# Whole and half tiles in two expert layers, early mixture tiles beside the row scatters, and a transposing load of the mixture's rows

## What is computed

```python
gate = sigmoid(h @ Wh.T + z_t @ Wz.T + b)                 # recurrence over 256 steps
h = tanh(h * leak + gate * z_t)
mask = one_hot(top_k(softmax(xt @ gate_w + gate_b), 2)).sum(1)      # first expert layer, E = 8, F = 1024
x = x + einsum('eth,te->th', relu(xt @ w1[e] + b1) @ w2[e] + b2, mask)
shared = (silu(x @ sw1.T) * (x @ sw3.T)) @ sw2.T          # mixture: shared layer of 512
routed = sum over the top 2 of gate_e * gelu(x @ rw1[e].T) @ rw2[e].T     # 8 experts of 128
y = (shared + routed) / 3
x = x + quantised_ffn(y)                                  # scales from maxima over all tokens
```

## Time and profile before

| | |
|---|---|
| median of the runs | 1201.23 us |
| profiled execution | 1204.75 us, span 1202.9 us |
| TensorE | 1023.2 us busy (85%), weight loads 805.0 us |
| VectorE, ScalarE, GpSimd | 823.5, 548.2, 389.3 us busy |
| first expert layer | 377.6 to 790.3 us |
| router, shared units, row scatters | 790.3 to 912.6 us |
| mixture tiles | 912.6 to 1036.4 us |
| sum of results | 1036.4 to 1087.5 us |

### The profile page before, as it was taken

How to read it: one execution, slowest core, us unless ns; L and a number is a source line. 1 busy time by engine, 2 the same in 40 slices (tenths; PEclk the granted TensorE clock), 3 DMA queues, 4 the chain that set the end, 5 groups by cost and what they waited for, 6 DMA issues and landing times.

```text
span 1202.9 us, 30907 instructions
## 1 busy us (share of the span) xinstructions
PE 1023.2 (85%) x10073; PEld 805.0 (67%) x10085; DVE 823.5 (68%) x2840; ACT 548.2 (46%) x1736; POOL 389.3 (32%) x428
## 2 busy tenths in 40 slices
PE   6777777777777999999999999967678999667898
PEld 5656656566565888888888888854355787433355
DVE  5676777776776778985555555528664777777887
ACT  4555555555554333333333333343425767114376
POOL 1002112111123666243333333315773667202000
PEclk9999999999999999999999999979898999978999
DMA  8313323233233578555444443374246998530024
GB/s 231 102 58 103 90 89 103 83 99 102 76 107 107 88 140 165 101 84 67 66 66 57 62 64 60 59 200 161 89 140 207 281 291 280 198 121 0 1 36 105
DMA packets 127354, 136.49 MB, mean 113 GB/s; under 512 B 62337, under 2 KB 102146, under 8 KB 127042
## 3 DMA queue, kind: packets, MB, share of 16 engines
q1 hardware_dynamic: 104770, 93.34, 29.4%
q0 software_dynamic: 22464, 41.61, 15.3%
HBM read 74.43 MB, written 58.70 MB: 111 GB/s over the span
## 4 chain that ended last, share of the span: by engine, by line
PE 66%; DVE 14%; ACT 9%; issue 5%; POOL 3%; DMA 3%; SPq 0%; DVEq 0%; POOLq 0%; ACTq 0%
PE ps L1395 17%; PE ps L1405 17%; PE ps L646 10%; PE ps L2011 8%; DVE ps L1940 6%; PE ps L2016 5%; ACT work L1864 4%; ACT ps L1859 4%; POOL mrows L1331 2%; DVE imax L1253 2%; PE ps L1981 2%; PE ps L731 2%; PE ps L1162 1%; PE ps L1167 1%; PE ps L1133 1%
## 5 line engine op out<-in xcount | busy, mean ns | idle before, releaser
L1423 ACT ACTIVATE lane<-ps,b_now 128x256 f32<-128x256 f32 x312 | 147.6, 473 | 260.3 <-PE ps L1395 248.4
L1395 PE MATMUL ps<-lane,W 128*128 128x256 f16 x1872 | 213.1, 274 | 0.9 <-issue 0.9
L1405 PE MATMUL ps<-W,lane 128*128 x1872 | 210.7, 273 | 0.2 <-DVE lane L1498 0.2
L1395 PEld LDWEIGHTS ps<-lane,W 128*128 x1872 | 183.9, 98 | 24.0 <-issue 1.7
L1405 PEld LDWEIGHTS ps<-W,lane 128*128 128x128 f16 x1872 | 182.8, 98 | 22.1 <-issue 0.8
L1572 POOL DMA_INDIRECT results<-lane,dest x78 | 125.2, 1605 | 216.7 <-DVE lane L1486 180.5
L2011 PE MATMUL ps<-work 128*128 128x16 f16 x2048 | 98.8, 177 | 86.1 <-ACT work L1864 85.4
L2011 PEld LDWEIGHTS ps<-work 128*128 128x128 f16 x2048 | 76.1, 106 | 137.8 <-ACT work L1864 136.3
L1498 DVE TENSOR_TENSOR lane<-lane 128x256 f16<-128x256 f32 x312 | 133.1, 427 | 10.8
L1542 POOL DMA_INDIRECT rows<-work,slot_of x64 | 63.1, 987 | 156.4 <-DVE ps L1940 152.4
L1496 DVE CAST lane<-lane 128x256 f16<-128x256 f32 x312 | 93.5, 300 | 20.5 <-ACT lane L1423 20.5
(11 more groups left out here) (260 smaller groups left out, 1660.2 us busy)
## 6 DMA issues: line engine op xcount, KB each, us to landing
W<-mrows SPq DMA_DIRECT2D x39, 260.0 KB, 3.9
stage<-rweights SPq DMA_DIRECT2D x39, 256.0 KB, 3.7
stage<-in_w1T SPq DMA_DIRECT2D x16, 512.0 KB, 3.8
stage<-in_w2T SPq DMA_DIRECT2D x16, 512.0 KB, 4.1
b_now<-in_b SPq DMA_DIRECT2D x39, 128.0 KB, 2.9
work<-in_zT SPq DMA_DIRECT2D x32, 128.0 KB, 2.3
results<-in_xn SPq DMA_DIRECT2D x32, 128.0 KB
W<-results SPq DMA_DIRECT2D x8, 512.0 KB, 4.5
```

The source lines that it names most:

```text
L1395: last = pe.matmul(ps[:, f % 4, 0:ST], of_e(W1[:, bass.ds(e, 1), a, k, f * P:(f + 1) * P]), xT[:, p, b, k], start=(i == 0 and k == 0), sto ...
L1405: last = pe.matmul(ps[:, 4 + q, 0:D], hid[:, a, f, q * P:(q + 1) * P], of_e(W2[:, bass.ds(e, 1), b, f]), start=(i == 0 and f == 0), stop=( ...
L1423: act.activation(v4[:, f % 4], ps[:, f % 4, 0:ST], ACT.Relu, bias=b1_now[:, p, f:f + 1], scale=A_SCALE / W_SCALE).then_inc(l1_v, 1)
```

## The change

Both expert layers take 32 tiles of 256 rows and then 7 of 128 (`UNITS_MAX` = 71 half tiles of work, at most), the half ones written out after the loop; the table operations give each tile its room in units of 128 rows, 28 operations for the late part instead of 17, and the mixture uses the same two tables: the first 16 tiles after step 2, the rest three operations at a time among the tiles. Each group has its own row buffer. `mixT` is filled by a transposing DMA and `mtail` by a load of its own; the transposes on TensorE and their copy on ScalarE are gone. The pad writes stand in SP's tile loop behind tile 2. The steps hold 6, 9, 12 and 14 units, the tiles 45 (two per tile for the first seven, then one), 10 are behind. `x1` comes in 16 pieces, four in flight. The sum comes after all units, with two loads per group; the last group's shared outputs are read by ScalarE.

```diff
 PAIRS = 2 * N
-SLOT_TILES = (PAIRS + E * (ST - 1)) // ST
+HT = ST // 2
+UNITS_MAX = (PAIRS + E * (HT - 1)) // HT
+WHOLE_TILES = PAIRS // ST
+HALF_TILES = UNITS_MAX - 2 * WHOLE_TILES
+SLOT_TILES = WHOLE_TILES + HALF_TILES
 JOBS = 15
+LOOPED = (WHOLE_TILES - 2 - JOBS) // 2 * 2
 FIRST_JOB = 5
 EARLY = 16
...
+LATE = SLOT_TILES - EARLY
+LATE_WHOLE = WHOLE_TILES - EARLY
 BATCHES = TILES // RING
...
-STEP_UNITS = 8
-BRIDGE_UNITS = 12
-TILE_UNITS = 30
-LATE = 6
-COMBINE = (0, 1, 2, 6, 3, 4, 5, 7)
+STEP_AT = (0, 6, 15, 27, 41)
+TAIL_UNIT = UNITS * GROUPS - 10
+PADS_AT = 2
...
 
 
...
-        EARLY_OPS, LATE_OPS = 11, 17
...
+        EARLY_OPS, LATE_OPS = 11, 28
...
+        def is_half(n):
+            return isinstance(n, int) and n >= WHOLE_TILES
+
+        def blocks_of(n):
+            return 1 if is_half(n) else SQ
...
-                v = STEP_UNITS * m
                 for g in (2 * m, 2 * m + 1):
                     router(g)
-                for k in range(3):
-                    shared(v + k)
+                for v in steps_units(m, 0, 3):
+                    shared(v)
                 mix_ranks(m)
...
-            for v in range(STEPS_M * STEP_UNITS, FIRST_TILE_UNIT):
-                shared(v)
-
-            def tile_transposes(n):
-                pe.wait_ge(mrow_in[n % ROW_BUFS], 16 * (n // ROW_BUFS) + 16)
-                if n:
-                    pe.wait_ge(mT, n)
-                rows_ = mrow[:, n % ROW_BUFS].bitcast(F16)
-                for c in range(2 * DC):
-                    for q in range(SQ):
-                        last = pe.transpose(psh(0)[:, c * ST + q * P:c * ST + (q + 1) * P],
-                                            rows_[:, q, c * P:(c + 1) * P], identh[:])
-                last.then_inc(mT_ps, 1)
+                if m < STEPS_M - 1:
+                    transposes(2 * m + 2)
+                for v in steps_units(m, 3, 5):
+                    shared(v)
+                if m < STEPS_M - 1:
+                    transposes(2 * m + 3)
+                for v in steps_units(m, 5):
+                    shared(v)
...
-                pe.wait_ge(mT, n + 1)
+                pe.wait_ge(mT_in[n % ROW_BUFS], 16 * (n // ROW_BUFS) + 16)
...
-                split_matmul(ps[:, 1 + n % 2, 0:ST], lambda s, k: mw1[:, n % ROW_BUFS, s, k],
-                             lambda s, k: mxT[:, n % 2, s, k], range(DC)).then_inc(m1_ps, 1)
+                split_matmul(ps[:, 1 + n % 2, 0:P * blocks_of(n)], lambda s, k: mw1[:, n % ROW_BUFS, s, k],
+                             lambda s, k: mixT(n)[:, s, k], range(DC)).then_inc(m1_ps, 1)
...
-                if n < SLOT_TILES - 1:
-                    tile_transposes(n + 1)
                 tile_first(n)
...
-                b = g % XBUFS
-                act.wait_ge(x_in[g % 2], 16 * (g // 2) + 16)
-                if g >= XBUFS:
-                    act.wait_ge(moved[b], 2 * GT * 16 * (g // XBUFS))
-                act.activation(xsn[:, b, :, 0:D], x1[:, GT * g:GT * g + GT], ACT.Copy, scale=A_SCALE).then_inc(xn_hi, 1)
-                at = C_TOKEN + GT * g
-                act.activation(xrow[:, b, :, D:D + 1], cst[:, at:at + GT].rearrange("p (q a) -> p q a", a=1), ACT.Copy,
+                for i in (2 * g, 2 * g + 1):
+                    h = slice(2 * (i % 2), 2 * (i % 2) + 2)
+                    act.wait_ge(x_in[i % 4], 16 * (i // 4) + 16)
+                    act.activation(xrow[g // 4][:, g % 4, h].bitcast(F16)[:, :, 0:D], x1[:, 2 * i:2 * i + 2], ACT.Copy,
+                                   scale=A_SCALE).then_inc(xn_hi, 1)
...
-                v = STEP_UNITS * m
-                mix_route_op(dve, m, 0)
-                shared(v)
...
-            mix_table(dve)
-            for v in range(STEPS_M * STEP_UNITS, FIRST_TILE_UNIT):
-                shared(v)
+                u = steps_units(m)
+                if m == 0:
+                    ops(m, 0, MIX_OPS)
+                    input_lo(2)
+                    for v in u[0:2]:
+                        shared(v)
+                    input_lo(3)
+                    for v in u[2:]:
+                        shared(v)
+                else:
+                    ops(m, 0, 1)
+                    shared(u[0])
+                    ops(m, 1, 9)
+                    shared(u[1])
+                    ops(m, 9, 15)
+                    shared(u[2])
+                    ops(m, 15, MIX_OPS)
+                    if m < STEPS_M - 1:
...
+                    else:
+                        dve.wait_ge(router_step, MIX_OPS * STEPS_M)
+                        dve.tensor_copy(mends[:], base[:]).then_inc(ends_ready, 1)
...
+                if m == STEPS_M - 2:
+                    dve.wait_ge(router_step, MIX_OPS * (STEPS_M - 1))
+                    for n in range(EARLY_OPS):
+                        early_table_op(dve, n, mix_tables)
...
+            def late_tables(n):
+                for k in range(3 * n, min(3 * n + 3, LATE_OPS)):
+                    late_table_op(dve, k, mix_tables)
...
+                late_tables(n)
             tile_out(SLOT_TILES - 1)
-
-            def combine(at):
-                g, b = COMBINE[at], at % TILE_BUFS
-                yg = y[:, GT * g:GT * g + GT]
-                if g < LATE:
...
+            for v in range(TAIL_UNIT, UNITS * GROUPS):
+                shared(v)
+            for g in range(GROUPS):
+                yg, b = y[:, GT * g:GT * g + GT], g % TILE_BUFS
+                if is_last(g):
+                    dve.wait_ge(out_read, GT * GROUPS)
+                for k in range(2):
+                    dve.wait_ge(routed_in[k][b], 16 * (g // TILE_BUFS) + 16)
+                    link(dve, dve.tensor_tensor(yg, yg, routed[b][:, :, k], ALU.add))
                 dve.tensor_reduce(ymax[:, g:g + 1], yg.rearrange("p q d -> p (q d)"), AX.X, ALU.max).then_inc(combined, 1)
...
-                pool.wait_ge(router_step, MIX_OPS * (g // 2 + 1))
-                pool.wait_ge(xn_lo, g + 1)
-                pool.wait_ge(tok_set, g + 1)
+                m = g // 2
+                pool.wait_ge(router_step, MIX_OPS * (m + 1))
...
+                            .then_inc(moved[m], 16)
...
-            with eng.Fori(0, (SLOT_TILES - 2 - JOBS) // 2) as i:
+            with eng.Fori(0, LOOPED // 2) as i:
...
-            for n in range(SLOT_TILES - 2, SLOT_TILES):
+            for n in range(JOBS + LOOPED, SLOT_TILES):
...
-                            last = pe.matmul(ps[:, f % 4, 0:ST],
-                                             of_e(W1[:, bass.ds(e, 1), a, k, f * P:(f + 1) * P]), xT[:, p, b, k],
+                            last = pe.matmul(ps[:, f % 4, 0:wide],
+                                             of_e(W1[:, bass.ds(e, 1), a, k, f * P:(f + 1) * P]), xrows[:, b, k],
...
-                        for q in range(SQ):
+                        for q in range(blocks_of(n)):
...
+                blocks = rows_d.rearrange("r (q p) n -> (r q) p n", q=SQ)[bass.ds(r, blocks_of(n))]
+                sp.dma_start(xg_tail[:, p, 0:blocks_of(n)], blocks[:, :, D - 1:D + 1].rearrange("q p n -> p q n"))\
                   .then_inc(xg_in[p], 16)
...
+                sp.dma_start_transpose(rows_T(n, p).rearrange("p s k n -> p (s k) n"),
+                                       blocks.rearrange("q p n -> (q p) n")[:, 0:D].bitcast(F16)).then_inc(xT_in[p], 16)
...
-                sp.dma_start(x1[:, GT * g:GT * g + GT], results_d[GN * g:GN * g + GN].rearrange("(q p) d -> p q d", p=P))\
-                  .then_inc(x_in[g % 2], 16)
-
...
+                half = slice(2 * i, 2 * i + 2)
+                sp.dma_start(x1[:, half], results_d[2 * P * i:2 * P * (i + 1)].rearrange("(q p) d -> p q d", p=P))\
+                  .then_inc(x_in[i % 4], 16)
+
...
+            def pad_rows_out():
+                rows_flat = mrows_d.rearrange("r s n -> (r s) n")
+                sp.wait_ge(ends_ready, 1)
+                for e in range(E):
+                    end = sp.value_load(mends[0:1, e:e + 1], min_val=0, max_val=ROOMS * ST - ST)
+                    sp.dma_start(rows_flat[bass.ds(end, ST)], pads_d[e]).then_inc(padded, 16)
...
+                if n == EARLY:
+                    sp.wait_ge(mtable_ready, 2)
+                    sp.wait_ge(spare_rows, 16)
+                    sp.wait_ge(padded, 16 * E)
+                    sp.wait_ge(moved[STEPS_M - 1], 4 * GT * 16)
...
-                    sp.wait_ge(mT_ps, n - ROW_BUFS + 1)
+                    sp.wait_ge(m1_ps, n - ROW_BUFS + 1)
...
-                sp.dma_start(mrow[:, b], mrows_d[bass.ds(r, 1)].rearrange("a (q p) n -> p (a q) n", p=P))\
-                  .then_inc(mrow_in[b], 16)
+                src = mrows_d.rearrange("r (q p) n -> (r q) p n", q=SQ)[bass.ds(r, blocks)]
+                sp.dma_start(mtail[:, b, 0:blocks], src[:, :, D:].rearrange("q p n -> p q n")).then_inc(mtail_in[b], 16)
+                sp.dma_start_transpose(mixT(n).rearrange("p s k n -> p (s k) n"),
```

(46 more changed lines are left out.)

515 lines of the change are left out of this document (263 added, 252 removed).

## The result

The changed kernel takes 1192.58 us (median of 4 runs, 1192.31 to 1192.92); the kernel before took 1200.87 in the same session. The ratio is 0.9931, 95% interval 0.9914 to 0.9948: 8 us faster, where I had forecast 43, and outside my range of 1138 to 1183. The profiled execution took 1192.59 us with a span of 1190.7, 12.2 us under that of before. The expert layer now ends at 765.7 us, 24.6 earlier than before, so to set a later event of after beside one of before, or beside my prediction, add 24.6.

The account below looks back on a forecast made before the run. TensorE was taken to bound the expert layer, and SP's queue the mixture's tiles after the change. Half tiles' 36.1 us plus 7.2 from the sum's earlier end made 43.3 off 1201.2: 1158 us, range 1138 to 1183.

Parts of the forecast that it names:

- Part 1: First expert layer: seven half tiles at 5.3 us, 56 ns per 128-column matmul, save 36.1 us (18 to 36).
- rival D: Half tiles' first layer doesn't shrink (matmuls up to 109 ns, or engines behind can't follow): 1176 us, chance 0.08.
- Part 2: Seam to the mixture: one last scatter and smaller x1 pieces let router 0 start 3 us earlier.
- Part 3: Tiles overlapping the row scatters: only 48 scatters needed, at 1.33 us each; first row load at 880, 32 us earlier.
- Part 4: Transposing load in the mixture's tiles: SP becomes the bound, 3.68 us per whole tile; tiles end 10 us later.
- Rival A: Mixture's tiles: the transpose doesn't hold SP up and engines bound the tiles: 1113 us, chance 0.12.
- C: Mixture's tiles: transposes above 2.6 us each make the kernel slower than before; at 3.0 us, 1213 us; chance 0.04.
- B: Mixture's tiles: transposes slow down under load, whole ones 1.9 us on average: 21 us more, 1179 us, chance 0.14.
- Part 5: Sum of results behind the tiles: 29.3 us of operations, ending at 1080.3 against 1087.5, 7.2 us earlier.
- The bad ends that my sum names: Range terms in us: crowding 12, half transpose 3, tail clock 8, step before the tiles 5, Part 1 up to 18.

Follow-up runs that it names:

- experiment 1: The changed kernel with the half tiles' first-layer weights at a fixed address (expert 0) instead of one from a register: 1189.39 us.
- experiment 2: The changed kernel with the seven half tiles taking turns with the last seven whole ones: 1189.78 us.
- experiment 3: The weights' write earlier: at tile 14 in the changed kernel, 1194.54 us; at tile 29 with half tiles in turns with whole ones, 1188.48 us.
- experiment 4: The changed kernel with the routing operations of steps 1 and 2 ahead of the shared layer's reads: 1187.68 us.
- experiment 5: The changed kernel with all 64 row scatters awaited before the first row load, instead of 48: 1224.28 us.
- experiment 7: The changed kernel with the mixture tiles' weights, from tile 4 on, loaded from ScalarE's queue instead of SP's: 1176.32 us.
- experiment 9: The changed kernel with the transposing load undone: one plain load of rows, transposes on TensorE and a copy on ScalarE: 1170.97 us.
- experiment 6: The changed kernel with the eight pad writes issued from ScalarE's queue behind tiles 0 to 7, instead of by SP: 1199.25 us.
- experiment 8: The changed kernel with early routing operations and weights from ScalarE's queue: 1170.47 us; second version, with the pads on ScalarE as well: 1184.45 us.

## Why the prediction was wrong

The forecast was 43 us, the change brought 8. The mechanism that I called the heart, SP's queue as the bound of the tiles, held; four steps took longer than my sum had them, by 12.1 (half tiles), 3.6 (seam), 8.8 (start of the rows) and 6.6 us (SP's time for the tiles).

**Part 1, failed: the price of a 128-column matmul.** "56 is the line continued": the transposes that I took for the row nearest to the half tile's matmuls have their weights at fixed addresses and come eight at a time. A matmul with an expert's weights has its address worked out by TensorE's sequencer, two register operations for every three matmuls. The whole tiles have the same 32 operations, and their 48 matmuls still take 5.24 us: at 109 ns each the sequencer has time for them and gets ahead. From the second half tile on it hasn't, and 48 matmuls take 4.3 us instead of 2.7 (experiments 1 and 2). 24.0 us saved, not 36.1, inside the bounds of 18 to 36 that I had written down and then left. That is nearest to rival D, to which I had given a chance of 0.08, but D had other causes for it: addresses stand nowhere in my prediction. They explain most of the miss and not all; with fixed ones 6.8 of the 12 us come back. By the rule that I had set aside (the Trainium skill, TensorE: Matmul & The Clock Gate, section Back-to-back issue gap, 81 ns sustained for 128 columns) this step would have lost 8 us; the trace has 90 ns in the six tiles, and the stage lost 12.1 us. But experiment 1 has 59 ns with the same 48 pairs, so it is not the columns that make 90: the rule's figure came near by another road.

**Part 2, wrong by 3.6 us, then right.** The seam from the last matmul to router 0 takes 18.6 us (before 18.0), not 15.0. The write of the weights was issued 9.7 us before the end of the expert layer in the kernel before, and 6.6 us before it now; it takes 9.4 us to land, and so falls among the last scatters. With the write at tile 14 the seam got 1.3 us of this back (experiment 3). Smaller pieces of x1 brought 0.2 us in the chain, not 0.8. From router to first row scatter it is 8.8 us; I had 8.7.

**Part 3, wrong by 8.8 us.** The rows start 20 us earlier than before (867.8 + 24.6 = 892.4 against 912.6), not 32. I let 47 scatters run at 1.33 us without a stop. POOL's own pace is 1.27, but it waited 6.4 us for the slots of step 2. The tables came 3.7 us behind the issue of the last of the 48 scatters, and SP loaded the first weights and then the first rows behind them, 6.2 us behind that scatter, where I had 3.4. I had looked at step 0's order on VectorE and not at steps 1 and 2, which kept the old one; putting them first brought 7 us (experiment 4). TensorE's granted clock in this stage was 0.82, where before had 0.89, and from 843 us on twelve matmuls of 512 columns took 5.2 us, 432 ns each instead of 211; what the clock itself cost here was not tested apart. That TensorE would have finished the steps by 885 to 890 in the clock of before was wrong as well: the first tile's matmul is at 888.6 in after's, 913 in before's. It cost nothing, because the pads kept SP busy meanwhile.

**Part 4, the heart: right in mechanism, 6.6 us short.** SP bounds the tiles (experiments 5, 7 and 9): 161.6 us from first rows to last weights against my 155 (the terms add up to 156). The transposes of half tiles at 1.22 us and not 0.8 are 3 us of the difference, and crowding the rest: whole tiles at 4.00 us, not 3.84. Of its terms one was right by luck: the pads' 11.2 us are in the sum, and without them SP waits 11.0 (experiment 6). A sum over one queue holds only where the queue never waits; where I write a term I must also ask what the queue would do without it. Rival A (not held up) and C (over 2.6 us a transpose) are out; B too: the median is 1285 ns.

**Part 5, right.** From the last weights' issue to the end of the sum it took 45.4 us; by my steps, 1080.3 - 1035 = 45.3. The sum itself ran from 1045.5 to 1074.8, the 29.3 us that I had.

All four errors lie on one side, and most are places where I took the hopeful end: 36 of 18 to 36, 3 us gained at the seam, scatters without gaps. The bad ends that my sum names (12, 3, 8, 5 and 18) add up to 46 us, which would have held the time at 1204; my range had 25, as if they could not come together. The start of the rows alone went past its 5.

## What to carry to other kernels

Before work is moved from an engine to a transposing DMA, add up what the issuing queue spends on a tile: here 1.3 us of issue and a second load on SP made a queue that had been a helper the bound, and the plain load with transposes on TensorE was 24 us faster. When tiles get smaller, what was hidden behind a matmul comes out, here the sequencer's address arithmetic; putting small tiles between large ones hid most of it. And a write placed "at the end" moves with the end: look at what it then meets.

## What the runs showed of the hardware that I had not expected

- With a weight address from a register, 48 matmuls of 128 columns take 4.3 us, with a fixed one 2.8; 32 register operations of 46 ns, 1.5 us, lie between them. Directly behind a whole tile it is 3.0 to 3.2 us.
- A transposing load of 128 rows holds SP nearly as long as one of 256: 1.22 us against 1.28. Single ones took up to 2.0 us in the changed kernel, 2.5 in experiment 6 and 3.5 in the second version of experiment 8.
- Beside one 2 MB write from SBUF to DRAM a scatter takes twice as long to land: 7.8 to 8.9 us against 3.8.
- With transposing loads and the weights on ScalarE's queue (experiment 7) the DMA engines are full (1.02) at 231 GB/s; with plain ones (experiment 9) they are at 0.79 with 240 GB/s.
- A register load and a DMA issue on ScalarE's queue between two dependent activations stop it 1.3 us (experiment 6).
